# One half of a batch's shared network moved behind the routed experts, with the guards off `tensor_scalar` and new instruction lists

## The chip, the cores and the metric

The kernel runs on one core of one Trainium2 chip. The metric is the device time of one execution in microseconds (us); lower is better. Before the change the median of three runs is 598.0 us (597.97 to 598.31).

## What is computed

`x` holds four batches (B = 4) of 512 tokens with 512 features. Two layers follow one another, each behind a layer norm and each added back to `x` with the tanh of a gate:

```python
x = x + tanh(g_xattn) * expert_forward(layernorm(x), fside, ctx)     # per batch, weights of its own
x = x + tanh(g_ffn)   * moe(layernorm(x), gate_w, w_gate, w_up, w_down, ws_gate, ws_up, ws_down)

def expert_forward(xe, guw, dw):          # twice a "smooth quant" linear: int8 steps per row
    gate, up = split(smooth_quant_linear(xe, guw)); return smooth_quant_linear(silu(gate) * up, dw)

def moe(x):                               # T = 2048 tokens, E = 16 experts, top 2, capacity 256, I = 352
    w, idx = top_k(softmax(x @ gate_w.T), 2)
    y  = for each expert: (silu(buf @ w_gate) * (buf @ w_up)) @ w_down, rows added back with w
    sh = (silu(x @ ws_gate) * (x @ ws_up)) @ ws_down                  # the shared network, IS = 704
    return y + sh
```

In the smooth-quant linear the maxima over columns give `s = sqrt(max(amax_x, eps) / max(amax_w, eps))`, the maxima over rows give the step sizes `max(row_max, eps) / 127`, and `eps` is 1e-6.

## The kernel before

Every engine has a program of its own, a list of calls that is written out by hand; nothing reorders it. Semaphores tie the lists together: a call waits at its head, and everything behind it on that engine waits with it. So the order of these five lists is the schedule.

**Stage A, the quantised layer (calls that end in `_a`, `_b`, `w`, `w2`, with a batch number first).** For a batch `a`, PE turns weights and tokens into the PSUM banks `ps_a` (`turn_w`, `turn_x`), DVE reduces their maxima (`amax_w`, `amax_x`), `ratio_a`, POOL's `root_a` and `smooth_a` make the smoothing, `scale_x` (DVE) and `scale_w` (POOL, 128x2048) apply it, `x_steps` and `w_steps` make the steps, ACT quantises (`quant_x`, `quant_w`) and moves the turned integers (`ints_x`, `ints_w`), and PE multiplies (`product_a`, `dequant_a` on DVE behind it). The second linear repeats this in `ps_d` with half the width (`turn_w2`, `turn_g`, `root_b`, `scale_g`, `scale_w2`, `product_b`, `dequant_b`). `add_x`, `stats_b`, POOL's `norm_b` and ACT's `normalise_b` then give the batch's second layer norm `y`, which is stored to `x2n_scratch` and turned (`turn_y`, `x_hi`, `x_lo`) for the router (`logits`, `turn_logits`, `top_two`, ...). `stats_a(a)` on DVE and `norm_a(a)` on POOL are the first layer norm of batch `a`. POOL also makes the low parts of the shared weights (`split_gu_lo`, `split_d_lo`).

**The guards.** The three `max(.., eps)` are `tensor_scalar` instructions on 2 or 4 columns: in `ratio` (L1065, `recip_w`), in `smoothing` (L1086) and in `step_size` (L1100, `x_step` from PSUM, `w_step` from SBUF).

**Full precision.** A product in float32 is made of three in a reduced form: `three` issues hi*hi, hi*lo and lo*hi. So each weight and each activation is split into a high part (ACT) and a low part (DVE or POOL).

**The shared network.** It goes by half-batches of 256 tokens, `shared_up(b, h, m, g)` and `shared_down(b, h, m, k)` in six chunks m (five of 128 columns of IS, one of 64 in which gate and up share one product). A half is 11 calls of `shared_up` with 12 matmuls of 256 columns each, and 12 calls of `shared_down` (10 with 3 matmuls of 512 columns, 2 with 2). Behind each chunk stand `shared_silu` and `shared_hi` on ACT and `shared_hid` and `shared_lo` on DVE. Six halves, (0,0) to (2,1), are woven into stage A by the lists. Where PE would have nothing to do, `keep_busy(n)` issues n matmuls that nobody reads (L1752).

**The experts.** When the routing tables are ready (`index`), POOL gathers an expert's tokens (`gather`), PE turns them (`turn_tokens`, L1938), and 16 equal steps follow: three `up` of 24 matmuls of 256 columns, three `down` of 6 of 512 columns, one `turn_tokens`. SP may load expert 1's weights only when all shared up-products are done (`sp.wait_ge(sh_gu, CHUNKS)`), since they lie over the shared weights.

**The tail.** The two halves of the last batch run as four more steps of the same kind, E to E + 3: the shared weights are loaded in two parts of 352 columns as if they were two experts (E and E + 1 in the weight buffers), and each part is multiplied with each half (`weights_of`). `shared_rows(e)` on DVE adds each step's rows to `x2`. When all expert rows are in `expert_out_scratch`, POOL's `gather_rows(b, k)` fetches them for each batch (L554, 8 gathers per batch), `add_rows(b, half)` on DVE adds them (L1666, L1671), and SP stores `x2` (L396).

Of the kernel before, what the change touches and what calls it, by code (L numbers as in the profile page):

```python
# [24 lines left out]
def flamingo_block(nc, x, guw, dw, g_x, g_f, gate_w, w_gate, w_up, w_down, s_gate, s_up, s_down, out):  # L25
# [63 lines left out]
    slot_col = place(cur, "slot_col", [P, 2, J, 2], U32)  # L89
# [102 lines left out]
    HALVES = 2 * (B - 1)  # L192
    CHUNKS = MS * HALVES
    NE, NW = E + 4, E + 2

    def weights_of(e):

        return e if e < E else E + (e - E) // 2
# [13 lines left out]
    with ExitStack() as ctx:  # L212
        def sem(name):
# [47 lines left out]
        slot_cols, got_in, sum_half, summed, out_done = (  # L261
            sem("slot_cols"), [[sem(f"got_in{k}_{half}") for half in "ab"] for k in range(3)], sem("sum_half"), sem("summed"), sem("out_done"))
# [23 lines left out]
        def _(sp):  # L286
# [98 lines left out]
            load_tokens(E, 0)  # L385
# [11 lines left out]
            sp.wait_ge(out_done, 16 * 2 * B)  # L397
# [3 lines left out]
        def _(pool):  # L401
# [4 lines left out]
            pool.memset(ln_eps[:], LN_EPS).then_inc(const_ready, 1)  # L406
            pool.memset(zeros[:], 0.0).then_inc(const_ready, 1)
# [8 lines left out]
            pool.wait_ge(const_ready, 11)  # L416
# [9 lines left out]
            def norm(b, done, mean, var, var_eps, rstd, mean_rstd, shift):  # L426

                pool.tensor_tensor(var_eps, var, ln_eps[:], ALU.add).then_inc(done, 1)
# [5 lines left out]
                pool.tensor_tensor(shift, zeros[:], mean_rstd, ALU.subtract).then_inc(done, 1)  # L434
# [19 lines left out]
            def root_a(a):  # L454
                root(LA, a, C)
# [33 lines left out]
            root_a(0)  # L489
            norm_a(1)  # L490
            scale_w(0)
            norm_a(2)
            split_gu_lo(0)
            norm_a(3)
            split_gu_lo(1)
            split_gu_lo(2)
            split_gu_lo(3)
            split_d_lo(0)
            root_b(0)
            split_d_lo(1)  # L500
# [1866 lines left out]
```

## Time and profile before

| | before |
|---|---|
| median of 3 runs | 598.0 us |
| the profiled execution | 599.84 us |
| its span, first to last instruction | 598.1 us |
| mean granted clock of TensorE | 0.981 of full speed |
| PE, DVE, ACT, POOL busy | 94%, 70%, 50%, 26% |
| experts' steps, matmuls of 256 columns | about 282 ns each as shown |

The profile shows each instruction with its own length; matmuls overlap one another, so the distance from one step to the same place in the next tells PE's pace, and the mean of one matmul doesn't. An idle engine is shown with what released it. The chain of waits follows the end of the span back, step by step.

### The profile page before, as it was taken

What the parts mean: (1) busy time and instruction counts of PE and PEld (TensorE: products, weight loads), DVE (VectorE), ACT (ScalarE), POOL (GpSimd) and SP (SyncE); (2) the same over time, 40 slices, a digit from 0 to 9 for tenths busy, and PEclk for the clock granted to TensorE, in tenths of its full rate; (3) what the DMA queues carried; (4) which work ended last, traced back from release to release, by engine and by line L of the source; (5) the groups of instructions that cost most, each with busy time, mean ns of one, the idle gap of its engine ahead of it and who ended that gap; (6) DMA issues with size and microseconds to landing.
All of it is one profiled execution on the core that took longest, in us unless ns stands there. A gap on an engine that the chain in (4) does not pass through costs nothing.

```text
span 598.1 us, 10333 instructions
## 1 busy us (share of the span) xinstructions
PE 560.9 (94%) x3949; PEld 478.8 (80%) x3949; DVE 415.8 (70%) x755; ACT 296.1 (50%) x460; POOL 156.9 (26%) x157
## 2 busy tenths in 40 slices
PE   7977989999998999999998999999999999999991
PEld 3544647988896888888887899999999999999980
DVE  4868796997899757566826766665666666666586
ACT  3175574386338541543146556556556666653110
POOL 2469510231041101010041222222232220006772
PEclk9979899999999999999999999999999999999995
DMA  7911021013001120011076667777777765755686
GB/s 261 385 48 64 13 94 71 2 36 141 1 2 37 70 98 2 1 71 50 2 243 188 216 219 239 232 261 239 248 248 231 232 215 181 231 206 154 199 279 241
DMA packets 45460, 89.01 MB, mean 149 GB/s; under 512 B 4256, under 2 KB 24736, under 8 KB 44400
## 3 DMA queue, kind: packets, MB, share of 16 engines
q1 hardware_dynamic: 40304, 71.74, 35.5%
q0 software_dynamic: 5120, 16.78, 9.2%
q8 instruction: 24, 0.39, 0.3%
q14 instruction: 12, 0.10, 0.1%
HBM read 71.73 MB, written 16.78 MB: 148 GB/s over the span
## 4 chain that ended last, share of the span: by engine, by line
PE 66%; DVE 14%; POOL 6%; DMA 5%; issue 4%; ACT 4%; SPq 1%; POOLq 0%; DVEq 0%; ACTq 0%
PE ps_gu L1710 12%; PE ps_gu L1711 11%; PE ps_gu L1712 11%; POOL got L554 5%; PE ps_d L1710 5%; PE ps_d L1711 5%; PE ps_d L1712 5%; PE ps_a L1938 2%; PE ps_d L1731 2%; DMA raw_d<-in_L_ffn_w_down 2%; PE ps_a L1731 2%; PE ps_a L1799 2%; DMA w<-in_ctx 2%; PE ps_gu L1752 1%; DVE xn L1119 1%
## 5 line engine op out<-in xcount | busy, mean ns | idle before, releaser
L1710 PE MATMUL ps_gu<-ex_xhi,w_hi 128*128 128x256 f32 (+1 forms) x480 | 136.9, 285 | 1.7 <-DVE w_lo L1321 1.7
L1711 PE MATMUL ps_gu<-ex_xlo,w_hi 128*128 128x256 f32 (+1 forms) x480 | 135.0, 281 | 0.0
L1712 PE MATMUL ps_gu<-ex_xhi,w_lo 128*128 128x256 f32 (+1 forms) x480 | 134.8, 281 | 0.0
L1710 PEld LDWEIGHTS ps_gu<-ex_xhi,w_hi 128*128 128x128 f32 (+1 forms) x480 | 86.3, 180 | 6.7 <-issue 5.6
L1711 PEld LDWEIGHTS ps_gu<-ex_xlo,w_hi 128*128 128x128 f32 (+1 forms) x480 | 86.1, 179 | 1.2
L1712 PEld LDWEIGHTS ps_gu<-ex_xhi,w_lo 128*128 128x128 f32 (+1 forms) x480 | 86.3, 180 | 0.0
L1710 PE MATMUL ps_gu<-xt_hi,sw_hi 128*128 128x256 f32 x264 | 78.7, 298 | 1.0 <-DVE sh_hid L1293 1.0
L1711 PE MATMUL ps_gu<-xt_lo,sw_hi 128*128 128x256 f32 x264 | 74.4, 282 | 0.0
L1712 PE MATMUL ps_gu<-xt_hi,sw_lo 128*128 128x256 f32 x264 | 74.4, 282 | 0.0
L1321 DVE TENSOR_TENSOR w_lo<-raw_gu,w_hi 128x1408 fp32r<-128x1408 f32 x36 | 58.2, 1616 | 1.1 <-DMA x2n_scratch<-y 1.1
L1710 PEld LDWEIGHTS ps_gu<-xt_hi,sw_hi 128*128 128x128 f32 x264 | 50.0, 190 | 5.4 <-DVE sh_hid L1293 1.7
L934 ACT ACTIVATE ex_silu<-ps_gu 128x256 f32<-128x256 f32 (+1 forms) x60 | 22.5, 375 | 60.5 <-PE ps_gu L1712 60.5
L525 POOL DMA_INDIRECT xg<-x2n_scratch,idx_col x32 | 47.1, 1473 | 17.6 <-POOL idx_col L521 12.7
L1710 PE MATMUL ps_d<-wd_hi,ex_hhi 128*128 128x512 f32 (+1 forms) x120 | 47.7, 398 | 3.7 <-DVE ex_hlo L1606 3.7
L1711 PEld LDWEIGHTS ps_gu<-xt_lo,sw_hi 128*128 128x128 f32 x264 | 50.2, 190 | 1.1
L938 ACT ACTIVATE ex_hhi<-ex_hid 128x256 fp32r<-128x256 f32 (+1 forms) x60 | 25.1, 418 | 50.7 <-DVE ex_hid L1603 50.7
L1712 PEld LDWEIGHTS ps_gu<-xt_hi,sw_lo 128*128 128x128 f32 x264 | 50.2, 190 | 0.0
L1752 PE MATMUL ps_gu<-ident_b 128*128 128x512 bf16 x157 | 44.9, 412 | 3.6 <-POOL fold L424 3.6
L1712 PE MATMUL ps_d<-wd_hi,ex_hlo 128*128 128x512 f32 (+1 forms) x120 | 47.6, 397 | 0.0
L1711 PE MATMUL ps_d<-wd_lo,ex_hhi 128*128 128x512 f32 (+1 forms) x120 | 47.5, 396 | 0.0
L1606 DVE TENSOR_TENSOR ex_hlo<-ex_hid,ex_hhi 128x256 fp32r<-128x256 f32 (+1 forms) x60 | 25.4, 424 | 30.9 <-ACT ex_hhi L938 30.9
L741 ACT ACTIVATE w_hi<-raw_gu 128x2816 fp32r<-128x2816 f32 x18 | 45.8, 2547 | 0.3 <-DMA raw_d<-in_L_ffn_w_down 0.3
(217 smaller groups left out, 1129.3 us busy)
## 6 DMA issues: line engine op xcount, KB each, us to landing
raw_gu<-in_L_ffn_w_gate SPq DMA_DIRECT2D x16, 704.0 KB, 4.5
raw_gu<-in_L_ffn_w_up SPq DMA_DIRECT2D x16, 704.0 KB, 6.0
raw_d<-in_L_ffn_w_down SPq DMA_DIRECT2D x16, 512.0 KB, 7.3
expert_out_scratch<-eo SPq DMA_DIRECT2D x16, 512.0 KB, 7.5
w<-in_fside_BxS2xS SPq DMA_DIRECT2D x4, 1024.0 KB, 5.2
x2n_scratch<-y SPq DMA_DIRECT2D x4, 1024.0 KB, 3.8
out<-x SPq DMA_DIRECT2D x8, 512.0 KB, 4.7
x<-in_x SPq DMA_DIRECT2D x1, 3072.0 KB, 16.7
```

The costliest lines, as they stand in the source:

```text
L525: pool.indirect_dma_start(xg[q][:, h, :], None, x2n_dram, bass.IndirectOffsetOnAxis(idx_col[:, q, h:h + 1], 0)).then_inc(xg_in[q], 16)
L554: pool.indirect_dma_start(got[k][:, j, n, :], None, eo_dram, bass.IndirectOffsetOnAxis(slot_col[:, b % 2, j, n:n + 1], 0)).then_inc(got_in ...
L741: act.activation(w_hi[q][:], raw_gu[q][:], ACT.Copy).then_inc(ex_whi, 1)
L934: act.activation(ex_silu[0:k, (q + m) % 2, :], ps_gu[0:k, (q + m) % 2, 0:CAP], ACT.Silu).then_inc(ex_sg, 1)
L938: act.activation(ex_hhi[0:k, m, :], ex_hid[0:k, (q + m) % 2, :], ACT.Copy).then_inc(ex_hi, 1)
L1321: dve.tensor_tensor(w_lo[q][:, g], raw_gu[q][:, g], w_hi[q][:, g].bitcast(F32), ALU.subtract).then_inc(ex_wlo, 1)
L1606: dve.tensor_tensor(ex_hlo[0:k, m, :], ex_hid[0:k, (q + m) % 2, :], ex_hhi[0:k, m, :].bitcast(F32), ALU.subtract).then_inc(ex_lo, 1)
L1710: pe.matmul(dst, a_hi, b_hi, start=start, stop=False)
L1711: pe.matmul(dst, a_hi, b_lo, start=False, stop=False)
L1712: return pe.matmul(dst, a_lo, b_hi, start=False, stop=stop)
L1731: last = pe.transpose(dst[:, j * P:(j + 1) * P], src[:, j, c * P:(c + 1) * P], ident[:])
L1752: pe.matmul(ps_gu[:, 1, :], ident_b[:], ident_b[:].unsqueeze(1).broadcast_to((P, J, P)), start=True, stop=True)
```

## The change

What it does:

- The shared network's half (2,0) leaves the lists of stage A. It is done behind the experts, with the last batch's two halves: `TAIL = [(2,0), (3,0), (3,1)]`. Five halves stay in stage A.
- The tail goes by half-batch: for each of three halves the two parts of the weights follow one another and add up in the same PSUM banks, so that the tail has six steps, and `shared_rows` adds each half's rows once instead of twice.
- The last batch's expert rows are added row tile by row tile, ahead of the last half's shared rows, and its output is stored in four parts.
- The guards are `scalar_tensor_tensor` with a second operand (`ones`, or a constant tile with 1/127) in place of `tensor_scalar`.
- The slot columns of all batches are copied once, ahead of the row gathers.
- The lists of all engines are new, with 135 matmuls in `keep_busy` where there were 157.

```diff
-    HALVES = 2 * (B - 1)
+    TAIL = [(B - 2, 0), (B - 1, 0), (B - 1, 1)]
+    HALVES = 2 * B - len(TAIL)
...
-    NE, NW = E + 4, E + 2
+    NE, NW = E + 2 * len(TAIL), E + 2
...
+            def at_least_eps(dst, src, factor):
+
+                return dve.scalar_tensor_tensor(out=dst, in0=src, scalar=Q_EPS, in1=factor, op0=ALU.max, op1=ALU.mult)
...
-                link(dve.tensor_scalar(w, sm["amax_w"][:, 0:width], Q_EPS, None, ALU.max))
+                link(at_least_eps(w, sm["amax_w"][:, 0:width], ones[:, 0:width]))
...
-                return dve.tensor_scalar(small[layer][which + "_step"][:], row_max, Q_EPS, 1.0 / QMAX, ALU.max, ALU.mult)
+                return at_least_eps(small[layer][which + "_step"][:], row_max, inv_qmax)
...
             root_a(0)
+            scale_w(0)
+            split_gu_lo(0)
             norm_a(1)
-            scale_w(0)
+            split_gu_lo(1)
             norm_a(2)
...
+            def last_rows():
+
+                t = len(TAIL) - 1
+                b, h = TAIL[t]
+                dve.wait_ge(ex_d, M * NE)
+                dve.wait_ge(sum_last, HALF)
+                for k in range(HALF):
+                    j = HALF * h + k
+                    dve.scalar_tensor_tensor(out=x2[:, b, j, :], in0=ps_d[:, 2 * (t % 2) + k, :], scalar=tg[:, 1:2],
+                                             in1=x2[:, b, j, :], op0=ALU.mult, op1=ALU.add).then_inc(summed, 1)
...
+            for t in range(len(TAIL)):
+                for w in range(2):
+                    tail_up(t, w, 0)
+                    if w:
+                        tail_down(t, 0, 2)
+                    elif t:
+                        tail_down(t - 1, 1, 2)
+                    else:
+                        down(E - 1, 1, 2)
+                    tail_up(t, w, 1)
+                    tail_down(t, w, 0)
+                    if w and t + 1 < len(TAIL):
+                        turn_tokens(E + t + 1, E // 2, (t + 1) % 2)
+                    tail_up(t, w, 2)
+                    tail_down(t, w, 1)
+            tail_down(len(TAIL) - 1, 1, 2)
```

DVE's list at the first batch's stage A, from the first maxima to the first steps (`bn_a` is `stats_a`, `amax_w_b` is `amax_w2`). Before:

```order
L1035 TENSOR_REDUCE amax_w_b<-ps_d 128x1 x2
L1035 TENSOR_REDUCE amax_x_a<-ps_a 128x1 x4
L1088 RECIPROCAL rsmooth_a<-smooth_a 128x4
L1012 BN_STATS bn_a<-x_49 128x6 x4
L1119 TENSOR_TENSOR xn<-xn,ps_a 128x2048
L1097 TENSOR_REDUCE ps_a<-xn 128x4
L1100 TENSOR_SCALAR x_step_a<-ps_a 128x4
L1012 BN_STATS bn_a<-x_49 128x6 x4
L1097 TENSOR_REDUCE w_max_a<-w_120 128x4
L1100 TENSOR_SCALAR w_step_a<-w_max_a 128x4
```

The same place in the changed kernel:

```order
L1035 TENSOR_REDUCE amax_x_a<-ps_a 128x1 x4
L1092 RECIPROCAL rsmooth_a<-smooth_a 128x4
L1123 TENSOR_TENSOR xn<-xn,ps_a 128x2048
L1101 TENSOR_REDUCE ps_a<-xn 128x4
L1063 SCALAR_TENSOR_TENSOR x_step_a<-ps_a,consts 128x4
L1101 TENSOR_REDUCE w_max_a<-w_118 128x4
L1063 SCALAR_TENSOR_TENSOR w_step_a<-w_max_a,consts 128x4
L1035 TENSOR_REDUCE amax_w_b<-ps_d 128x1
L1012 BN_STATS bn_a<-x_49 128x6 x4
```

The maxima of `w2` and the statistics of batches 1 and 2 now stand behind the first steps, and the guards have another form.

DVE's list at the very end (`x_49` is the result `x2`, `got_172` is a batch's gathered rows, `ex_hid` and `ex_hlo` belong to the last step's last chunk). Before:

```order
L1603 TENSOR_TENSOR ex_hid<-ex_silu,ps_gu 96x256
L1606 TENSOR_TENSOR ex_hlo<-ex_hid,ex_hhi 96x256
L1666 SCALAR_TENSOR_TENSOR x_49<-got_174,wts,x_49 128x512 x2
L1671 SCALAR_TENSOR_TENSOR x_49<-got_174,wts,x_49 128x512 x2
L1657 SCALAR_TENSOR_TENSOR x_49<-ps_d,tg,x_49 128x512 x2
L1666 SCALAR_TENSOR_TENSOR x_49<-got_172,wts,x_49 128x512 x2
L1671 SCALAR_TENSOR_TENSOR x_49<-got_172,wts,x_49 128x512 x2
```

The same place in the changed kernel:

```order
L1594 TENSOR_TENSOR ex_hid<-ex_silu,ps_gu 96x256
L1597 TENSOR_TENSOR ex_hlo<-ex_hid,ex_hhi 96x256
L1665 SCALAR_TENSOR_TENSOR x_49<-got_170,wts,x_49 128x512
L1668 SCALAR_TENSOR_TENSOR x_49<-got_170,wts,x_49 128x512
L1665 SCALAR_TENSOR_TENSOR x_49<-got_170,wts,x_49 128x512
L1668 SCALAR_TENSOR_TENSOR x_49<-got_170,wts,x_49 128x512
L1659 SCALAR_TENSOR_TENSOR x_49<-ps_d,tg,x_49 128x512 x2
```

Before, the last batch's gathered rows came behind the last shared rows (twice the last two lines); now the shared rows come last.

## Rows read from the trace of the kernel before

**Rows 1.** Stages: us, PE, PEld, DVE, ACT, POOL busy (x), PEclk, DMA, GB/s.

```profile
0.00:101.20 101.20, 84.05 (x490) 49.80 (x490) 75.04 (x133) 53.22 (x74) 45.15 (x51) 0.95 0.39 139
101.20:278.30 177.10, 174.45 (x1302) 151.36 (x1302) 137.08 (x299) 87.73 (x163) 25.57 (x22) 1.00 0.12 43
278.30:309.50 31.20, 30.66 (x224) 26.37 (x223) 19.37 (x65) 9.26 (x18) 6.56 (x9) 1.00 0.22 67
309.50:530.50 221.00, 217.58 (x1563) 201.76 (x1562) 139.02 (x186) 128.68 (x173) 43.53 (x39) 1.00 0.72 234
530.50:598.10 67.60, 54.12 (x375) 49.51 (x374) 45.32 (x73) 17.24 (x32) 36.12 (x36) 0.91 0.63 199
```

**Rows 2.** The chain of waits in order of time: start us, us, what.

```profile
322.47 1.53 DVE w_lo L1321
...
348.38 0.87 PE ps_a L1938 x8
...
525.55 0.89 PE ps_a L1938 x8
```

**Rows 3.** Timeline of DVE in stage A: start us, us, engine, line, instruction.

```profile
13.86 1.34 DVE L1035 TENSOR_REDUCE amax_w_b<-ps_d 128x1 f32<-128x512 f32 x2 [0.69 <-PE ps_d L1731]
...
20.86 2.47 DVE L1012 BATCH_NORM_STATS2 bn_a<-x 128x6 f32<-128x512 f32 x4
...
31.43 2.25 DVE L1097 TENSOR_REDUCE w_max_a<-w 128x4 f32<-128x2048 f32 x1
...
33.71 2.84 DVE L1100 TENSOR_SCALAR w_step_a<-w_max_a 128x4 f32<-128x4 f32 x1
...
55.56 2.75 DVE L1065 TENSOR_SCALAR recip_w_b<-amax_w_b 128x2 f32<-128x2 f32 x1
...
123.24 3.04 DVE L1301 TENSOR_TENSOR sh_hlo<-sh_hid,sh_hhi 128x256 fp32r<-128x256 f32 x1
```

**Rows 4.** Timeline of POOL in stage A.

```profile
25.62 4.53 POOL L463 TENSOR_TENSOR w<-w,line_a 128x2048 f32<-128x2048 f32 x1
...
33.38 3.15 POOL L475 TENSOR_TENSOR sw_lo<-raw_sgu,sw_hi 128x1408 fp32r<-128x1408 f32 x1
...
51.68 6.61 POOL L482 TENSOR_TENSOR sd_lo<-raw_sd,sd_hi 128x2560 fp32r<-128x2560 f32 x1
...
121.38 4.62 POOL L463 TENSOR_TENSOR w<-w,line_a 128x2048 f32<-128x2048 f32 x1 [5.27 <-ACT line_a L625]
```

**Rows 5.** Timeline of ACT in stage A.

```profile
23.25 0.60 ACT L625 ACTIVATE line_a<-ps_a 128x512 f32<-128x512 f32 x1 [7.84 <-PE ps_a L1746]
...
39.74 1.36 ACT L590 ACTIVATE sw_hi<-raw_sgu 128x1408 fp32r<-128x1408 f32 x1
...
92.48 2.93 ACT L607 ACTIVATE xn<-x,shift_a,rstd_a 128x512 f32<-128x512 f32 x4
```

**Rows 6.** Timeline of all engines where the experts begin.

```profile
298.38 0.18 DVE L1283 CAST idx<-r_tmp 128x32 uint32<-128x32 f32 x1
...
304.92 1.09 PE L1938 MATMUL ps_a<-ident,xg 128*128 128x128 f32 x8 [0.54 <-DMA xg<-x2n_scratch,idx_col]
...
309.51 0.38 PE L1710 MATMUL ps_gu<-ex_xhi,w_hi 128*128 128x256 f32 x1
```

**Rows 7.** Timeline of the tail: up-products, gathers, last chunk, last sum (first and last).

```profile
530.53 0.36 PE L1710 MATMUL ps_gu<-ex_xhi,w_hi 128*128 128x256 f32 x1
...
541.06 0.97 POOL L554 DMA_INDIRECT got<-expert_out_scratch,slot_col  x1 [0.84 <-POOL slot_col L549]
...
580.78 0.28 PE L1712 MATMUL ps_gu<-ex_xhi,w_lo 128*96 128x256 f32 x1
...
583.96 0.42 DVE L1606 TENSOR_TENSOR ex_hlo<-ex_hid,ex_hhi 96x256 fp32r<-96x256 f32 x1 [0.48 <-ACT ex_hhi L938]
...
586.83 1.14 POOL L554 DMA_INDIRECT got<-expert_out_scratch,slot_col  x1 [0.30 <-issue]
...
593.49 1.42 DVE L1671 SCALAR_TENSOR_TENSOR x<-got,wts,x 128x512 f32<-128x512 f32 x2
```

More of the change, by code:

```diff
@@ L503, in _ @@
             scale_w(1)
+            split_gu_lo(2)
             norm_b(0)
+            split_d_lo(0)
+            split_gu_lo(3)
+            split_d_lo(1)
+            norm_a(3)
+            root_b(1)
             root_a(2)
-            root_b(1)
             scale_w2(1)
@@ L977, in _ @@
             for e in range(E + 1, NE):
-                for m in range(M):
-                    hidden(e, e % 2, m, False)
+                t = (e - E) // 2 + 1
+                hidden(e, e % 2, 0, False)
+                hidden(e, e % 2, 1, False)
+                if e % 2 and t < len(TAIL):
+                    tokens(E + t, t % 2)
+                hidden(e, e % 2, 2, False)
         @block.vector
@@ L1988, in _ @@
             turn_g(0, 1)
-            keep_busy(6)
+            turn_w(1, 3)
+            keep_busy(4)
             turn_x(1, 0)
@@ L2009, in _ @@
             product_b(0, 1)
+            keep_busy(5)
+            turn_qx(1, 0)
             keep_busy(1)
@@ L2017, in _ @@
             row_w(1)
-            keep_busy(7)
+            keep_busy(1)
             turn_qw(1, 0)
@@ L2099, in _ @@
-            turn_y(1, 3)
-            shared_down(0, 0, 4, 0)
-            turn_w(3, 2)
-            shared_down(0, 0, 4, 1)
-            logits(1)
-            turn_w(3, 3)
-            shared_down(0, 0, 5, 0)
-            turn_x(3, 0)
-            turn_logits(1)
+            shared_down(0, 0, 5, 1)
+            turn_x(3, 0)
+            shared_up(0, 1, 3, 0)
+            table(0)
+            shared_up(0, 1, 3, 1)
+            turn_w2(2, 0)
+            shared_down(0, 1, 0, 0)
+            turn_w2(2, 1)
@@ L2166, in _ @@
+            turn_y(2, 1)
+            product_a(3, 0)
+            turn_y(2, 2)
+            shared_down(1, 0, 0, 1)
+            turn_y(2, 3)
+            shared_down(1, 0, 1, 0)
+            product_a(3, 1)
+            logits(2)
+            product_a(3, 2)
+            turn_logits(2)
+            shared_down(1, 0, 1, 1)
             product_a(3, 3)
-            turn_y(2, 1)
+            rank(1)
             shared_up(1, 0, 5, 0)
-            turn_y(2, 2)
             shared_up(1, 1, 0, 0)
-            turn_y(2, 3)
+            shared_down(1, 0, 2, 0)
```

882 lines of the change are left out of this document (420 added, 462 removed).

## The prediction

> **What bounds the kernel now.** I read busy time by stage first, then the chain of waits, then timelines at the places that the new lists change.
>
> There are four stages [rows 1]; the edges at 101.2 and 278.3 us are the first and the last batch's `turn_logits`. Up to 101.2 us PE is busy 84 us, but much of that is `keep_busy`: this is the latency of stage A's first batch, before any shared product can start. From there to 309.5 us PE is busy 205 of 208 us. From 309.5 us the experts, again PE alone, with DVE at 63%. At 530.5 us the last expert's step is over but for one down-product, and the tail begins.
>
> PE's pace comes from the chain: from 348.38 to 525.55 us there are 13 experts' steps [rows 2], so 13.63 us each, of which the turn of the tokens is 0.87. The other 12.76 us are 72 matmuls of 256 columns and 18 of 512, 108 units of 256 columns, so **0.118 us a unit**. The 282 ns that the profile gives a matmul is its length, not its pace.
>
> The end isn't PE's. The tail's last up-product is at 580.9 us [rows 7], but POOL is still issuing gathers until 588, and DVE's last sum ends at 594.9, 3.2 us ahead of the span's end [rows 1, 7]. From 530.5 us to the end pass 67.6 us.
>
> **The tail grows.** A half in the tail is two parts of 108 units, 25.5 us, and 0.87 for turning its tokens where it isn't the first. Before, the tail's up-products took 50.4 us [rows 7], which is 4 x 12.76 + 0.87 less the last 1.38 of down-products: no stall in it. With six steps it is 6 x 12.76 + 2 x 0.87 - 1.38 = 76.9 us. Behind it come the last chunk's hidden values (about 2.0 us, an estimate: four instructions like the 0.42 of `ex_hlo`, three gaps up to its 0.48), the last batch's row tiles 2 and 3 (four sums, two of which take 1.42 by the last row of [rows 7], with a wait between the two of a tile: 3.0), the last shared rows (1.4) and the same 3.2 for the store: 9.7. So the end lies 86.7 us behind the start of the tail instead of 67.6: **+19.1 us**. The 32 gathers, issued from 541.06 to 588 [rows 7], are covered by PE's own work now; that is why 26.4 us more on PE lengthen the tail by 19.1 only. Were they late after all, DVE would stop ahead of `hidden` and PE with it; they have some 8 us in hand, since the last gather should land some 60 us into the tail and its first sum stands 68 us into it. The single copy of the slot columns takes three copies off POOL under that cover: nothing. The extra load of tokens on SP (512 KB) stands behind the experts' stores and ahead of the output: nothing.
>
> **Stage A loses one half.** `shared_up` of a half is 132 units, `shared_down` 34 matmuls of 512 columns, 68 units: 200 units, 23.6 us, in a stretch that PE fills. The lists pull `turn_x` of batch 2 (12 turns of 0.11) from in front of this stretch into it: +1.4. So **-22.2 us** if PE stays as full as it is. It won't quite. DVE is busy 137 of the 177 us up to 278.3 [rows 1], and with a half less it has about 5 us less work in 22 less. The PE idle that this adds isn't in the trace: its bounds are 0, and all 22.2 (DVE and the latencies set the stretch already). The row nearest to it, PE 98.5% busy in the old lists, lies at the first end; I take 4.2.
> At the end of the stretch one wait can be counted. The routing needs about 13.5 us from the last `turn_logits` to the index, and 6.5 from the index to the turn of expert 0's tokens (298.38 to 304.92, [rows 6]). From the last `turn_logits` PE's old list had 255 units' worth, 30 us, the new one has 18, of which some 16 stand ahead of the turn. PE waits there 2.3 us more. Together +6.5.
>
> **The first batch's chain gets shorter.** In the new DVE list the first steps come at once [rows 3 to 5]:
> - `amax_w2` (two reductions) no longer stands ahead of `amax_x`: -1.3.
> - `scale_w(0)` on POOL began at 25.62 though ACT had copied its row at 23.85 [rows 5]: it stood behind `norm_a(1)`, which waits for `stats_a(1)` on DVE. Now -1.8. `w_max` began 1.3 behind its end, held by `stats_a(2)`: -1.3.
> - `w_step_a` took 2.84 us for four columns, until POOL's low part of the shared weights ended at 36.53. In the new POOL list nothing is on POOL then: -2.7. `recip_w_b` took 2.75, until 58.3, where POOL's 6.61 us ended: -2.6.
> - `split_gu_hi` (1.36) no longer stands ahead of `ints_w`, and fewer matmuls of `keep_busy` stand there: -1.7.
> - `silu_a(1)` and `normalise_a(2)`, which held the batch's last two turned chunks (92.48, 2.93 us), come behind them: -2.9. Small gains between: -0.4.
>
> The sum is **-14.7 us**, so the shared products begin near 85 us. What follows them is POOL's last `split_gu_lo`, due at the same time by the same rows, so there is little more to have here.
>
> **The guards.** `sh_hlo`, a `tensor_tensor` with two SBUF inputs and no fast form, took 3.04 us instead of 0.4 and ended at 126.28, just behind POOL's 4.62 us that ended at 126.00 [rows 3, 4]. So two SBUF inputs are enough to wait for POOL, and the new guard of `w_step` and `recip_w` has two. I give the new form nothing; the 5.3 us above come from the new order alone. `x_step` reads PSUM and never waited.
> The Trainium skill says the same (GPSIMD Engine Reference, Specifications and Key points): POOL shares its SBUF interfaces with VectorE, and instructions in a two-port mode or with two SBUF inputs contend. By a rule that only the two-port mode contends, every guard would be free, and the sum would be about 3 us lower, for one more stall, of 2.7, in the middle stretch; row and page speak against it.
>
> **Expert 1's weights.** They may be loaded when the shared up-products are over. Their low part ended at 324.0 [rows 2], while expert 0's step, 13.63 us from 309.51 less the 1.4 of its last down-product, would have let expert 1 start at 321.7. Since the 2.3 us wait above now lies behind the last up-product, this wait goes: **-2.3**.
>
> **Sum.** -14.7 - 22.2 + 6.5 - 2.3 + 19.1 = -13.6 us, so the span goes from 598.1 to 584.5 us. The profiled execution took 599.84, 1.74 more than its span: 586.2 after. The runs' median, 598.0, lies 0.3% below it, which gives **584.4 us**.
>
> **Rivals.**
> - *The lists are worse than they look: PE waits more in the middle stretch.* For: DVE at 77% there, tighter with less to fill; new POOL orders may put `scale_w` (4.6 us) over the guard of `w_step_b` in batches 1 to 3, up to 2.8 each, like the stall of `w_step_a` [rows 3]. Against: PE has other work queued for most of it. 9 us more: 593.
> - *The front doesn't get shorter* (a load or POOL's splits set it), but the middle does: without the 14.7 the time is 599.1, no change. For: POOL's `split_d_lo` and `split_gu_lo(3)` end only then. Against: each term is a row. A part of it is likelier than the whole.
> - *The middle stretch keeps its length, set by stage A's own latencies* (slower). The 22.2 us come back as PE idle, the tail's 19.1 stay, the front gives 14.7: -14.7 + 0 + 19.1 - 2.3 + 2.3 = +4.4, 602.4 us. It decides where PE's added idle passes 20 us. Against: PE is full there now, and DVE has 40 us free.
> - *More than I count*: no added idle in the middle and the wait for the tokens hidden: 578.
>
> **Chances.** Forecast as reckoned 0.55, better by 4 us or more 0.15, the first rival 0.17, the second 0.05, the third 0.06, something else slower 0.02. Below 0.2% a measurement of this kernel can't tell a difference. So faster 0.89, within 0.2% 0.03, slower 0.08. The range takes in the better case and most of the first rival: 576 to 596 us.
>
> **What the changed profile would show.** Right: the first `turn_logits` near 87 us; `w_step_a` at 0.2 us near 29; the first expert's matmul near 279; tail steps of 12.76 us without stalls; the last sums on DVE reading PSUM. Wrong: PE's share of 100 to 275 us clearly under 97%; a two-input guard of over 2 us on the chain; gathers still being issued when the last up-product ends; the first expert later than 290 us.

## The result, and the profile after

| | before | after |
|---|---|---|
| median of 19 runs each, us | 598.16 | 595.54 |
| lowest to highest | 597.73 to 600.37 | 593.04 to 597.62 |
| profiled execution: span, mean granted clock | 598.1, 0.981 | 595.7, 0.982 |

The ratio is 0.9951, with a 95% interval from 0.994 to 0.9962: faster, by 0.5% where 2.3% were forecast, 11.1 us above the forecast 584.4. On the four chips of all later runs the kernel before takes 609 us, and the changed kernel 616 on the one where it was repeated unaltered: there the change is a loss (`r_after` below).

The same five stages in the trace of the changed kernel, to set beside [rows 1]; columns: stretch, us, then busy us (and instructions) of PE, PEld, DVE, ACT, POOL, then the granted clock, DMA share, GB/s:

```profile
0.00:92.90 92.90, 75.43 (x456) 45.06 (x456) 71.08 (x128) 50.56 (x70) 44.18 (x49) 0.96 0.43 151
92.90:259.30 166.40, 163.41 (x1225) 140.11 (x1224) 134.65 (x297) 84.89 (x159) 27.75 (x26) 1.00 0.13 46
259.30:288.10 28.80, 22.39 (x149) 17.73 (x148) 15.71 (x57) 7.27 (x13) 7.44 (x9) 0.88 0.38 122
288.10:509.90 221.80, 218.83 (x1564) 203.03 (x1563) 140.82 (x188) 128.54 (x173) 46.26 (x40) 0.99 0.70 227
509.90:595.70 85.80, 79.83 (x563) 73.93 (x562) 50.99 (x84) 23.07 (x45) 35.41 (x32) 0.98 0.52 164
```

Against the forecast's stages: the front lasts 92.9 us instead of 86.5 (+6.4); from the first `turn_logits` to the first expert's matmul 195.2 instead of 192.7 (+2.5); the experts 221.8 instead of 218.7 (+3.1); the tail 85.8 instead of 86.7 (-0.9). These make up the 11.1. Three places hold the excess.

**The front: the stalls moved.** DVE's timeline of the changed kernel there (start us, us, engine, line, instruction), at the guards and the gating:

```profile
29.43 0.16 DVE L1063 SCALAR_TENSOR_TENSOR w_step_a<-w_max_a,consts 128x4 f32<-128x4 f32 x1
...
42.56 4.14 DVE L1178 TENSOR_TENSOR gated<-gated,xn 128x1024 f32<-128x1024 f32 x1 [0.56 <-ACT gated L668]
...
57.30 2.29 DVE L1063 SCALAR_TENSOR_TENSOR smooth_a<-root_a,ones 128x4 f32<-128x4 f32 x1
...
68.19 2.29 DVE L1101 TENSOR_REDUCE w_max_a<-w 128x4 f32<-128x2048 f32 x1 [0.44 <-POOL w L469]
...
70.51 0.81 DVE L1063 SCALAR_TENSOR_TENSOR w_step_a<-w_max_a,consts 128x4 f32<-128x4 f32 x1
```

And POOL's timeline at the same moments:

```profile
42.47 3.15 POOL L481 TENSOR_TENSOR sw_lo<-raw_sgu,sw_hi 128x1408 fp32r<-128x1408 f32 x1
45.58 1.18 POOL L434 TENSOR_TENSOR var_a<-mv_a,consts 128x4 f32<-128x4 f32 x1
...
57.24 2.34 POOL L475 TENSOR_TENSOR w<-w,line_b 128x1024 f32<-128x1024 f32 x1
...
68.13 3.17 POOL L481 TENSOR_TENSOR sw_lo<-raw_sgu,sw_hi 128x1408 fp32r<-128x1408 f32 x1
```

The first `w_step_a` is free now, as forecast (2.84 in [rows 3]). But the gating multiply, 1.2 us long in the three other batches, stands under the second `split_gu_lo`, and the guard of `smooth_a`, which had never waited before, under the scaling of the down weights. The multiply was long in the kernel before too, 2.10 us, so that 2.0 of its 2.9 us are new. Its line there:

```profile
50.71 2.10 DVE L1174 TENSOR_TENSOR gated<-gated,xn 128x1024 f32<-128x1024 f32 x1
```

Behind the multiply PE's granted clock is 0.50 from about 46 to 52 us. That isn't new either: in the kernel before it averages 0.66 from 34 to 44 us, behind the old stall of `w_step_a`.

`w_max_a`, a reduction with one input, ran its usual 2.29 us wholly under POOL's operation: not every instruction waits.

**The tokens of expert 0.** The chain there, in order of time:

```profile
273.65 2.10 POOL xg L531
276.06 6.17 DMA xg<-x2n_scratch,idx_col
282.27 1.97 PE ps_a L1957 x8
```

And the index on DVE and the loads on SP's queue, from the timeline:

```profile
272.22 0.18 DVE L1287 CAST idx<-r_tmp 128x32 uint32<-128x32 f32 x1
...
274.52 0.37 SPq L310 DMA_DIRECT2D raw_gu<-in_L_ffn_w_gate  x1
274.93 0.51 SPq L311 DMA_DIRECT2D raw_gu<-in_L_ffn_w_up  x1
275.48 0.51 SPq L314 DMA_DIRECT2D raw_d<-in_L_ffn_w_down  x1
276.03 0.83 SPq L316 DMA_DIRECT2D raw_d<-in_L_ffn_w_down  x1
```

The index is ready 12.9 us behind the last `turn_logits` (13.5 reckoned). But SP now asks for expert 1's weights at 274.5, 2.3 us behind the index, because the shared up-products end earlier against the routing; in the kernel before it asked at 303.7, 5.3 us behind. So the token rows share the DMA engines with the weights: 10.05 us from the index to the turn, not 6.5 [rows 6]. The windows show the second half of the bill (columns as above):

```profile
276.70:282.20 5.50, 0.40 (x2) 0.00 (x0) 0.00 (x0) 0.00 (x0) 2.41 (x4) 0.91 1.05 385
282.20:291.30 9.10, 9.03 (x30) 6.87 (x31) 4.29 (x5) 2.72 (x3) 2.10 (x3) 0.50 0.55 165
291.30:302.00 10.70, 10.38 (x78) 9.69 (x78) 4.37 (x8) 6.51 (x8) 2.44 (x2) 0.99 0.63 202
```

PE stands for 5 us, and the clock granted afterwards averages 0.50, 1.2 GHz, over 9 us.

**Expert 1's weights** are still waited for: `w_lo` at 302.07 is on the chain, as at 322.47 before [rows 2].

### The profile page after: what moved, and what is told of

Read it like the earlier page. It is cut to its first block, busy times and chain, and to the rows that moved or that the text cites. A ratio compares the mean times of both kernels' runs of the same rounds, so it can differ in the third digit from the quotient of the medians.

```text
span 595.7 us, 10318 instructions
## 1 busy us (share of the span) xinstructions
PE 559.9 (94%) x3949; PEld 479.9 (81%) x3949; DVE 413.2 (69%) x752; ACT 294.3 (49%) x460; POOL 161.0 (27%) x155
## 4 chain that ended last, share of the span: by engine, by line
PE 74%; DVE 15%; ACT 5%; POOL 2%; issue 2%; DMA 1%; DVEq 0%; POOLq 0%; ACTq 0%
PE ps_gu L1729 13%; PE ps_gu L1730 13%; PE ps_gu L1731 13%; PE ps_d L1729 6%; PE ps_d L1731 6%; PE ps_d L1730 6%; PE ps_a L1957 3%; PE ps_d L1750 2%; PE ps_gu L1771 2%; PE ps_a L1750 2%; PE ps_a L1818 1%; DMA xg<-x2n_scratch,idx_col 1%; ACT y L709 1%; PE ps_d L1818 1%; DVE pos_oh L1269 1%
## 5 line engine op out<-in xcount | busy, mean ns | idle before, releaser
L1729 PE MATMUL ps_gu<-ex_xhi,w_hi 128*128 128x256 f32 (+1 forms) x528 | 151.3, 287 | 1.3 <-DVE w_lo L1325 1.3
L1730 PE MATMUL ps_gu<-ex_xlo,w_hi 128*128 128x256 f32 (+1 forms) x528 | 149.3, 283 | 0.0
L1731 PE MATMUL ps_gu<-ex_xhi,w_lo 128*128 128x256 f32 (+1 forms) x528 | 148.8, 282 | 0.0
L1729 PE MATMUL ps_gu<-xt_hi,sw_hi 128*128 128x256 f32 x220 | 65.5, 298 | 0.0
L531 POOL DMA_INDIRECT xg<-x2n_scratch,idx_col x32 | 50.3, 1571 | 17.6 <-POOL idx_col L527 12.7
L1729 PE MATMUL ps_d<-wd_hi,ex_hhi 128*128 128x512 f32 x132 | 52.2, 395 | 2.1 <-DVE ex_hlo L1597 2.1
L1594 DVE TENSOR_TENSOR ex_hid<-ex_silu,ps_gu 128x256 f32<-128x256 f32 (+1 forms) x66 | 27.6, 419 | 35.4 <-ACT ex_silu L929 34.5
L1731 PE MATMUL ps_d<-wd_hi,ex_hlo 128*128 128x512 f32 x132 | 52.1, 395 | 0.0
L1730 PE MATMUL ps_d<-wd_lo,ex_hhi 128*128 128x512 f32 x132 | 52.0, 394 | 0.0
L561 POOL DMA_INDIRECT got<-expert_out_scratch,slot_col x32 | 35.4, 1106 | 59.8 <-DMA expert_out_scratch<-eo 50.3
L1341 DVE TENSOR_TENSOR ex_xlo<-ps_a,ex_xhi 128x1024 fp32r<-128x1024 f32 x19 | 23.3, 1224 | 34.1 <-ACT ex_xhi L761 34.1
```

What stands on the lines that cost most here:

```text
L531: pool.indirect_dma_start(xg[q][:, h, :], None, x2n_dram, bass.IndirectOffsetOnAxis(idx_col[:, q, h:h + 1], 0)).then_inc(xg_in[q], 16)
L561: pool.indirect_dma_start(got[k][:, j, n, :], None, eo_dram, bass.IndirectOffsetOnAxis(slot_col[:, b, j, n:n + 1], 0)).then_inc(got_in[k][ ...
L1594: dve.tensor_tensor(ex_hid[0:k, (q + m) % 2, :], ex_silu[0:k, (q + m) % 2, :], ps_gu[0:k, (q + m) % 2, CAP:2 * CAP], ALU.mult).then_inc(ex ...
L1729: pe.matmul(dst, a_hi, b_hi, start=start, stop=False)
L1730: pe.matmul(dst, a_hi, b_lo, start=False, stop=False)
L1731: return pe.matmul(dst, a_lo, b_hi, start=False, stop=stop)
```

## The experiments

Each kernel ran beside the kernel before on one chip, in five rounds. A run is called by the first part of its label (e1, f4, h2). All were run where the kernel before takes 608.5 to 609.8 us, so absolute times are not to be set against 595.5. The places where batches and experts pass can be, since up to the tail `r_after` repeats the first trace within 0.1 us. They are read from one trace of each run (starts on PE, us; medians and ratios are of all its executions):

| | first turn_logits | last | expert 0's tokens | expert 2's | tail's first | span's end | median | ratio to before |
|---|---|---|---|---|---|---|---|---|
| before, first chip | 101.1 | 278.3 | 304.9 | 334.5 | 525.4 | 598.1 | 598.2 | |
| after, first chip | 92.9 | 259.3 | 282.3 | 314.1 | 504.7 | 595.7 | 595.5 | 0.995 |
| r_before | 100.8 | 278.0 | 304.6 | 333.9 | 524.9 | 609.2 | 609.9 | 1.000 |
| r_after | 92.9 | 259.4 | 282.3 | 314.2 | 504.8 | 616.8 | 616.4 | 1.010 |
| e1 | 92.3 | 258.8 | 279.1 | 310.7 | 501.3 | 614.4 | 615.2 | 1.008 |
| e2 | 91.6 | 258.1 | 282.3 | 311.6 | 502.2 | 614.6 | 616.0 | 1.010 |
| e3 | 91.7 | 258.1 | 282.4 | 312.0 | 502.6 | 614.8 | 615.1 | 1.009 |
| e4 | 100.5 | 275.3 | 302.1 | 332.0 | 522.6 | 635.8 | 636.0 | 1.043 |
| e6 | 86.8 | 251.5 | 274.5 | 303.8 | 494.4 | 606.5 | 609.0 | 0.999 |
| e7 | 89.4 | 255.8 | 278.7 | 310.4 | 501.0 | 610.5 | 611.2 | 1.004 |
| e8 | 86.6 | 251.4 | 271.8 | 303.8 | 494.4 | 606.4 | 608.0 | 0.997 |
| f4 | 86.7 | 251.5 | 272.4 | 301.8 | 492.4 | 600.9 | 604.5 | 0.994 |
| f2 | 87.6 | 252.3 | 275.4 | 305.0 | 495.6 | 594.9 | 596.7 | 0.982 |
| f1 | 87.5 | 252.3 | 275.8 | 305.2 | 495.8 | 587.0 | 588.1 | 0.967 |
| h2 | 93.0 | 259.4 | 283.7 | 313.5 | 504.1 | 595.3 | 595.1 | 0.976 |
| h3 | 86.6 | 251.3 | 272.2 | 303.0 | 493.6 | 584.8 | 586.6 | 0.962 |
| h5 | 98.8 | 273.7 | 300.3 | 330.2 | 520.9 | 612.1 | 614.1 | 1.009 |

How far can one trace be trusted? The front's lists are the same in `r_after`, e1, e2 and h2, and their first `turn_logits` stands at 91.6 to 93.0; with e6's front it stands at 86.6 to 87.6 in six traces. From the last `turn_logits` to expert 2's tokens, a stretch that none of them alters, pass 53.9 to 54.8 us in `r_after`, e3, e7 and h2, and 52.3 to 52.9 in e6, f1 and f2. A difference of about 1 us between two traces shows nothing.

### The change itself on the second kind of chip: r_after, r_before

No edit.

> The changed kernel itself, unaltered, on the chip that the other runs of this call get. In the last four runs (on a chip where the kernel before takes 609.8 us, not 598.2) PE stood for 20 us in the tail between single matmuls, with nothing that it waited for, while the row gathers of batches 0 and 1 ran. Theory (the chip, or the moment, does it, and the four edits have no part in it): on the same kind of chip the unaltered change shows that stop as well, and its time there is above the kernel before's, some 612 us; where the kernel before takes 598, there is no stop and it takes 595.5. Rival (the edits shifted PE's code against the gathers): no stop in the unaltered change on any chip, 0.995 of the kernel before.

> The kernel before, unaltered, for its trace on this chip: the ratio is 1.000. Where the kernel before takes 609.8 us: the theory that PE stops for want of instructions while rows are gathered says that its extra 11.6 us lie in its tail, as one stop during a batch's gathers; the rival says that they are spread over the whole span (a slower memory), a few per cent of every stage that waits for DMA.

From the tail's first tokens to the end the changed kernel takes 91.0 us on the first chip and 112.0 here; the kernel before 72.7 and 84.3. The tail of `r_after` in windows:

```profile
504.78:520.50 15.72, 15.72 (x117) 14.70 (x116) 10.42 (x13) 8.25 (x12) 0.00 (x0) 1.00 0.58 194
520.50:537.60 17.10, 16.99 (x122) 15.66 (x120) 5.67 (x10) 4.90 (x9) 13.42 (x13) 1.00 0.63 182
537.60:556.90 19.30, 6.39 (x18) 3.98 (x17) 0.96 (x3) 1.06 (x3) 10.39 (x11) 0.58 0.60 173
556.90:616.80 59.90, 53.05 (x350) 48.27 (x350) 37.10 (x63) 10.25 (x24) 7.71 (x8) 0.93 0.30 106
```

And PE in the third of them:

```profile
543.82 0.37 PE L1731 MATMUL ps_gu<-ex_xhi,w_lo 128*128 128x256 f32 x1 [0.85 <-issue]
545.21 0.57 PE L1729 MATMUL ps_gu<-ex_xhi,w_hi 128*128 128x256 f32 x1 [1.02 <-issue]
546.61 0.37 PE L1730 MATMUL ps_gu<-ex_xlo,w_hi 128*128 128x256 f32 x1 [0.82 <-issue]
548.71 0.37 PE L1731 MATMUL ps_gu<-ex_xhi,w_lo 128*128 128x256 f32 x1 [1.72 <-issue]
```

The gathers begin at 520.5, one each 1.25 us, 24 without a pause. After 17 us of them PE starts recorded matmuls mostly only every 0.7 to 2 us instead of every 0.12, "issue" being idle time for which the profile shows no awaited event; it recovers at 556.9, some 5 us behind the last of the 24. So the edits don't do it, and the first theory holds: the chip or the moment does, and no run tells these two apart. In `r_before` it begins 22 us behind the first gather (540.5) and is shorter. The gathers there come in runs of eight with a pause of 1 us between them, which doesn't prevent it; its windows:

```profile
538.60:562.60 24.00, 24.00 (x175) 22.63 (x174) 9.52 (x15) 5.78 (x12) 17.09 (x19) 1.00 0.57 163
562.60:575.50 12.90, 6.29 (x20) 3.69 (x18) 4.99 (x8) 0.80 (x2) 7.58 (x8) 0.85 0.68 194
```

Which DMA queues moved anything during the stop of `r_after` (537.6 to 556.9), packets, MB, share:

```profile
q0 software_dynamic: 1023, 3.34, 60.1%
```

and in the same window of the changed kernel on the first chip, where PE is full:

```profile
q0 software_dynamic: 1063, 3.49, 65.2%
q1 hardware_dynamic: 282, 1.04, 13.5%
q8 instruction: 1, 0.02, 0.3%
```

So the gathers are about as fast here as there, and no queue moves instructions during the stop.

PE's slow starts are only half of it. ACT's timeline around the stop, on the first chip:

```profile
535.05 0.38 ACT L929 ACTIVATE ex_silu<-ps_gu 96x256 f32<-96x256 f32 x1 [1.80 <-PE ps_gu L1731]
```

and in `r_after`:

```profile
555.05 0.38 ACT L929 ACTIVATE ex_silu<-ps_gu 96x256 f32<-96x256 f32 x1 [20.23 <-remote]
```

In both PE starts the last product that this instruction needs at 534.7 to 534.8, before the slow starts. On the first chip ACT follows 0.3 us later, here 20.3. ACT itself isn't late: by the trace's semaphore records, of which some are missing, PE's signal for these products came at 555.02 (535.03 there). PE's next down-product needs what ACT and DVE make of them, and stands at 556.84 instead of 539.08. So PE's signals come late as well as its starts. The same wait is 20.4 us in e4 and in e6, 7.1 and 9.5 in `r_before`; in h2, with paced gathers, ACT follows within 2.6 us, and on the first chip within 1.6.

### Expert 1's weights behind expert 0's tokens: e1

```diff
             sp.wait_ge(sh_gu, CHUNKS)
+            sp.wait_ge(xg_in[0], 32)
             load_raw(1, 1)
```

> The changed kernel, with expert 1's weights asked for on SP only once expert 0's token rows have landed. Theory (the token rows and the 1.8 MB of weights share the DMA engines, and PE's idle 5.3 us let the clock fall): from the table of token indices being ready to the first token transpose about 6.5 us, as in the kernel before, in place of 10.05; PE idle under 2.5 us there; the granted clock stays 1.00 where it was 0.50 from 282 to 291; the first expert matmul 3.5 to 6 us earlier; the time 4 us below the changed kernel's 595.5, so 591.5 (590 to 593), unless the weights, which land some 4 us later, are then waited for at expert 1. Rival (the gather is slow by itself, its issues on POOL or its descriptors): the first token transpose still 9 us or more after the indices, the clock still at 0.50, and 595.5 to 599.

The gather lands after 3.46 us (6.17 unaltered), and the turn stands 7.35 us behind the index instead of 9.98: the contention is real. The clock didn't do as expected: it still averages 0.65 from 279 to 283 us and 0.75 from 283 to 291. Up to expert 2's tokens 51.9 us pass from the last `turn_logits`, 2.0 to 2.9 us less than in the four traces without the hold (53.9 to 54.8).

### Filler matmuls in the wait: e2

```diff
+            pe.wait_ge(sh_h, CHUNKS)
+            keep_busy(20)
             turn_tokens(0, 0, 0)
```

> The changed kernel, with 20 filler matmuls (0.21 us each, 4.3 us) on PE ahead of expert 0's token transposes; the weights are asked for where they were. Theory (half of what was lost at this place is the clock and not the wait): the tokens still arrive at the same time, 10 us after the indices, but the granted clock stays 1.00 from 282 to 291, where 9.3 us of work at 0.50 took twice its time; less what waits for ACT and DVE there, 3 us off, so 592.5 (591 to 594). Rival (the stretch is bound by the splitting of the tokens and by the weights of expert 1, so the clock costs nothing that the next waits don't hide): 595.5, within 1 us.

The clock from 282.2 to 291.3 us is 0.81 instead of 0.50, and expert 2's tokens come 53.5 us behind the last `turn_logits` instead of 54.8. But e3, which is without the filler, has nearly the same: its tokens come at the same 24.2 us, the clock of this window is 0.77, and expert 2's tokens stand at 53.9. So the filler's gain isn't shown, and neither are the 3 us expected of it; the median shows none. What e3 and `r_after` do show side by side, at the same edits here: with the clock at 0.77 the step from expert 0's tokens to expert 1's takes 12.8 us, at 0.50 it takes 15.1 (the loads were asked for 1 us earlier in e3, so not all of this need be the clock).

### The guards back as tensor_scalar: e3

```diff
-                return dve.scalar_tensor_tensor(out=dst, in0=src, scalar=Q_EPS, in1=factor, op0=ALU.max, op1=ALU.mult)
+                return dve.tensor_scalar(dst, src, Q_EPS, factor, ALU.max, *([ALU.mult] if factor else []))
...
```

> The changed kernel with its guards as tensor_scalar again, lists as they are. Theory (DVE's operation waits for the end of POOL's long one in either form, and the new lists have other guards under POOL's operations): the smoothing guards at 57.3 and 107.4 take 2.3 us as now, the first logits transpose is at 92.9 within 1 us, and the ratio to the changed kernel is 1.000 within 0.002. Rival (the new form waits less, and is what brought part of the 8.3 us of the front): two or more guards take 1 to 3 us that take 0.16 now, the first logits transpose at 95 or later, and 2 us or more slower than the changed kernel.

From the timeline of e3:

```profile
56.10 2.30 DVE L1063 TENSOR_SCALAR smooth_a<-root_a 128x4 f32<-128x4 f32 x1
```

2.30 us in the old form, 2.29 in the new one; the second `w_step_a` 0.81 and 0.80. The form is worth nothing in either direction. The front is 1.2 us shorter than in `r_after`, more than the 1 us expected, but so it is in e2, which has the new form: 91.6. The guards' times are the same; after the stall of the gating multiply the clock recovers earlier in both (48 to 53 us: 0.72 in e2 and e3, 0.54 in `r_after`).

### The lists of the kernel before: e4, and h5 with paced gathers

The changed kernel's tail, tables and guards, and the five lists of the kernel before without the moved half's parts:

```diff
-            shared_up(2, 0, 0, 0)
-            shared_down(2, 0, 0, 0)
-            shared_silu(2, 0, 0)
-            shared_hid(2, 0, 0)
...
```

> The move alone: the tail of the changed kernel (six steps, rows added once) and its guards, but PE, DVE, ACT, POOL and SP work through the lists of the kernel before, from which the twelve parts of the moved half-batch are struck. Theory (the first 101 us are paid by the new lists alone, and the moved half's work was what filled the waits of the middle): the first logits transpose stays at 101 us, where the new lists have 92.9; the middle loses 10 to 18 of its 177 us, the tail is 85.8; 602 us (599 to 607), slower than the kernel before. Rival (the move brings the gain and the new lists little): 596 or less.

> e4 (the new tail and guards with the lists of the kernel before, the moved half struck) with paced gathers. e4 took 636.0 us, 20 of them PE's stop; its tail began at 522.6, 2.8 us ahead of the kernel before's 525.4, where the new lists brought 20.7. Theory (with the old lists the struck work had filled waits, and the tail of 91 us is paid in full): 522.6 + 91 and what lies around the span, 615 (613 to 618); so the new lists are worth 18 to 19 us. Rival (part of e4's 636 is not the stop): 620 or more.

The middle stretch in the windows of e4:

```profile
100.50:275.30 174.80, 157.50 (x1143) 133.91 (x1148) 132.46 (x287) 82.68 (x150) 25.43 (x22) 0.95 0.13 43
```

The tail begins 2.8 us earlier than before, where some 22 us of PE's work were taken out: 17.3 of 174.8 us are PE idle now (2.7 before), at a clock of 0.95. The theory's 10 to 18 us off the middle didn't come; the stretch lost 2.3 (177.1 before). Without the stop, h5 takes 614.1, so the move alone costs 5.4 us even against a kernel before that loses some 11 to its own; with the new lists it is h2's 595.1, 19.0 us less.

### POOL's order in the front: e6, e7

```diff
             norm_a(1)
-            split_gu_lo(1)
             norm_a(2)
+            split_gu_lo(1)
```

e6 also has, in `scale_w2`:

```diff
                 pool.wait_ge(row_s_b_done, b + 1)
+                if b + 1 < B:
+                    pool.wait_ge(smooth_ready[LA], 2 * b + 4)
```

> The changed kernel with two edits on POOL's list: the low half of the second shared piece after the norm of batch 2 (in place of before it), and the scaling of the next down weights held until DVE has its smoothing factors. Theory (DVE's operations with two SBUF inputs wait for the whole of POOL's long operation, and these two waits are on the path of the first 93 us): the gating multiply at 42.6 takes 1.2 us in place of 4.14, the smoothing guards at 57.3 and 107.4 0.16 in place of 2.3; the first logits transpose 4 to 5 us earlier, at 88 to 89; 591 us (589.5 to 592.5). Rival (another chain, the weights' transposes on PE, ends in these stretches at the same time): the two operations are short, but the first logits transpose moves under 1.5 us, and 594 to 596.

> The changed kernel with only the first of e6's two edits: the norm of batch 2 ahead of the low half of the second shared piece, so that the gating multiply at 42.6 doesn't meet POOL's 3.15 us. e6 moved the first logits transpose from 92.9 to 86.8. Theory (the multiply's 2.9 us are paid with interest: PE was idle for 3.1 us and its clock at 0.50 from 46 to 53 us): the first logits transpose at 88.5 to 89.5, 4 us of the 6.1 from this edit, no stretch at 0.50 behind 44 us. Rival (each stall costs what it lasts and the rest came with the second edit): 90 to 90.5. The smoothing guard stays at 2.3 us in both.

From e6's timeline:

```profile
42.58 1.23 DVE L1180 TENSOR_TENSOR gated<-gated,xn 128x1024 f32<-128x1024 f32 x1 [0.57 <-ACT gated L670]
...
46.71 1.66 DVE L1065 SCALAR_TENSOR_TENSOR recip_w_b<-amax_w_b,ones 128x2 f32<-128x2 f32 x1
...
53.35 0.16 DVE L1065 SCALAR_TENSOR_TENSOR smooth_a<-root_a,ones 128x4 f32<-128x4 f32 x1
```

Both stalls are gone, and a guard that was free in the changed kernel (`recip_w_b`, 0.15 at 50.65) now waits 1.5 us under the operation that was moved.

The stretch from 48 to 53 us in the windows of `r_after`:

```profile
48.00:53.00 5.00, 5.00 (x21) 3.61 (x20) 2.78 (x7) 4.02 (x4) 1.07 (x3) 0.54 0.00 0
```

and in those of e7:

```profile
48.00:53.00 5.00, 3.91 (x26) 2.60 (x25) 4.70 (x13) 1.25 (x2) 1.74 (x3) 1.00 0.00 0
```

e7 brings 3.5 us (89.4 where 92.9 stood), inside the theory's range. But unaltered fronts stand at 91.6 to 93.0, so that it is 2.3 to 3.6, and theory and rival aren't told apart. Nor did the clock stay up: it averages 0.76 from 53 to 60 us, where `r_after` has 1.00. So what the half clock costs in the front is not shown. e6 brings 6.1 at the first batch (4.0 to 6.4 by the spread) and, by the guard at 107.4, another 1.7 in the middle (164.7 us from the first to the last `turn_logits` instead of 166.4).

### Both, and the weights held in part: e8, f4

e8 is e6 with e1's hold. f4 is e6 with:

```diff
-            load_raw(1, 1)
+            sp.dma_start(raw_gu[1][:, 0], wg_v[1]).then_inc(raw_in[1], 16)
+            sp.wait_ge(xg_in[0], 32)
+            sp.dma_start(raw_gu[1][:, 1], wu_v[1]).then_inc(raw_in[1], 16)
+            load_d(1, w_down[1])
```

> The two edits of e6 (POOL's order in the front) and the one of e1 (expert 1's weights asked for once expert 0's tokens are there) together. Theory (they act on stages one behind the other, so they add): first logits transpose at 86.8 and the last at 251.5 as in e6, the second expert's token transposes 33.7 us behind that (e1 had 34.2, the changed kernel 38.0), so 9 to 10 us below the changed kernel of this call: 586 us where that takes 595.5, if the tail has no stop. Rival (the hold of the weights costs expert 1 what it gives expert 0): 6 us below the changed kernel, as e6 alone.

> e6 with three of expert 1's four weight loads held until expert 0's token rows are there (the gate weights go out at once). e8 held all four: tokens 2.5 us earlier, but expert 1's own weights then 3.5 us later, and nothing left at expert 2. Theory (both need the same DMA bytes before expert 1 can start, so the order only shares the wait out): the third experts' token transposes 51 to 52.5 us behind the last logits transpose (52.3 in e6, 52.4 in e8), within 1.5 us of e6's time. Rival (the first load fills the DMA engines while POOL still writes the gather's descriptors, for free): 50 or less, 2 us or more below e6.

e8's rival was right: tokens 2.6 us earlier, and nothing left at expert 2 (52.4 us against 52.3 in e6). f4's rival was nearer than its theory: the tokens come nearly as early (272.4), and expert 2's stand 50.3 us behind, 2.0 us better than e6. h3, with the same hold, has 51.6, so the gain is 1 to 2 us: queueing one load early and three late keeps something of both.

### The gathers of the tail paced: f1, f2, h2, h3

```diff
             def gather_rows(b, k):
                 for j in range(J):
+                    pool.wait_ge(ex_d, M * E + 3 + 3 * (J * b + j) // 4)
```

That is f1, on e6; h2 has it alone on the changed kernel; h3 on f4. f2, on e6, has instead one wait ahead of batch 1's gathers (`M * E + 6`) and one ahead of batch 2's (`M * E + 10`).

> e6 (the changed kernel with POOL's two edits in the front) with the row gathers of the tail paced: each pair of gathers waits on POOL until PE has finished one more down projection, three in four of them, so that 2.5 us of gathers stand in every 3.2. Theory (PE's stop of 20 us comes from the unbroken run of 24 gathers; it began 17 us after the first of them in the unaltered change): with pauses no stop or one under 5 us, the tail from its first token transposes to the end 91 to 95 us in place of 112, and 590 (587 to 594) on a chip where the kernel before takes 609.7. Rival (the total of the gathers matters and not how closely they follow one another): the stop is as long and only later, 607 to 610.

> e6 with the row gathers in bursts: batch 1's eight wait for the seventh down projection of the tail and batch 2's for the eleventh, so that 5 us or more lie between one burst of 10 us and the next. Theory (unbroken run): as f1, no stop, since none of the bursts reaches the 17 us after which PE stopped; 590 (587 to 594). Rival 1 (each burst stops PE at a code page's end, by chance): one or two stops of 5 to 8 us, 597 to 605. Rival 2 (rows late for the sums): no stop, but DVE's adding of batch 2 or 3 waits and the end is 5 us later.

> The changed kernel with paced row gathers and no other edit. Theory (the stop in the tail is a thing by itself, and front, middle and experts stay as in the unaltered change): first logits transpose at 92.9, tail from its first token transposes 91 us in place of 112, 595 to 597 whatever the chip, so 0.978 of the kernel before where that takes 609, 0.995 where it takes 598. Rival (pacing also lengthens the tail where nothing stopped): 598 or more.

> The paced gathers, POOL's two edits in the front and expert 1's weights held but for the gate weights, together: f1 with f4's hold. Theory (stages one behind the other add): f1's 588.1 less the 2.0 us that f4 won up to the third experts' token transposes, 586 (585 to 587.5). Rival (the tail's first step meets something later, such as the last experts' stores, that gives it back): 588 or more.

The windows of f1, from the tail's first tokens:

```profile
495.80:518.90 23.10, 23.10 (x167) 21.54 (x166) 14.03 (x19) 11.31 (x18) 0.00 (x0) 1.00 0.41 139
518.90:570.00 51.10, 51.10 (x368) 47.85 (x367) 28.67 (x50) 11.13 (x25) 34.06 (x32) 1.00 0.69 208
570.00:587.00 17.00, 10.97 (x70) 9.32 (x68) 11.31 (x19) 2.02 (x5) 1.30 (x1) 0.88 0.33 120
```

All 32 gathers in 51 us, and PE full throughout. h2 takes 595.1 us where the kernel before takes 608.7, the same time as the change had on the first chip, so the stop was all that differed, and the pauses cost nothing. f2 has its longest stop at 566 us, where ACT's instruction came 4.7 us behind its products, late in the only run of 16 gathers left (550.7 to 572); its window:

```profile
565.00:575.00 10.00, 6.30 (x28) 4.89 (x27) 4.00 (x7) 1.54 (x4) 5.35 (x6) 0.72 0.79 238
```

That fits the length of the run. But in `r_before` the stop came although no run was longer than eight, with 1 us between them. So what is shown is that PE stopped 16 to 22 us into a stretch of dense gathers and that f1's pauses avert it; whether the unbroken run is what counts, or the rate of the gathers, is open. h3, with everything, takes **586.6 us**, 0.9624 of the kernel before (0.9608 to 0.964); it was tried only where that takes 609. It is the best version here.

## Why the prediction missed, point by point

- *The front, -14.7, measured -8.3.* The terms read from rows came (the first `w_step_a` 0.16 us at 29.43). The step that failed is the count of stalls: "the 5.3 us above come from the new order alone" took off the old ones and put in none. The new order adds 2.0 us at `gated` (4.14 where 2.10 stood), 2.1 at `smooth_a` and 0.65 at the second `w_step_a`, 4.8 of the missing 6.4; for the other 1.6 no cause is shown. One of the profile's signs of being wrong came with them, a two-input guard of over 2 us on the chain (`smooth_a`). With the two larger ones lifted and a new one of 1.5 in their place (e6), the first `turn_logits` stands at 86.8, where 87 was forecast.
- *The guards' form, nothing.* Right (e3). So is what the Trainium skill says under GPSIMD Engine Reference, Specifications and Key points, of two SBUF inputs: `gated` agrees, 4.14 us in place of 1.2.
- *The middle, -22.2 + 4.2.* PE's idle time there is 3.0 us in 166.4, after 2.7 in 177.1: hardly any was added, and 4.2 was too much. The work taken out came to what was reckoned: up to the first expert's matmul PE is busy 185.8 us instead of 205.1, and 22.2 us less if the 5.8 us that it worked at half clock (282.3 to 288.1) are counted as 2.9 (an estimate). The rival in which the stretch keeps its length is what e4 shows, with 17.3 us idle: it is the new lists that avert it.
- *The wait for the tokens, +2.3.* This is the term that fell furthest. The 6.5 us from index to turn were carried over, though the load of expert 1's weights had moved to the same moment; they became 10.05 (e1: 3.5 of DMA time instead of 6.2), and the half clock behind it was not in the sum at all. PE's idle time there grew by 5.9 us (6.4 of 28.8 us after 0.5 of 31.2), and the half clock takes some 2.9 more up to the first expert's matmul (the same estimate): 8.8 where 2.3 stood. With the 4.2 not needed, that leaves the 2.5 up to there, within some tenths. The 2.3 itself doesn't follow from the 20.0 us of routing and "some 16" of work that the text gives; the trace has 17.8 us of work there (259.3 to 277.1), which would give it.
- *Expert 1's weights, -2.3.* They didn't go: the load is asked for earlier, but tokens and weights need the same DMA engines, so that one wait split in two. The experts' 3.1 us above the forecast are mostly this 2.3; the last 3 us at half clock lie there too.
- *The tail, +19.1.* Right to 0.9 us on the first chip (85.8 against 86.7), the gathers covered (the last at 562.9, the last up-product at 586.4), the last sums on PSUM. Its four parts behind the last up-product add up to 9.6, not 9.7, which changes nothing. "Covered by PE's own work" was wrong on the others: there PE stops while POOL issues gathers without a pause, and the tail is 21 us longer; h2's pauses bring them back. No view of the first chip's trace shows it.

Rivals: the first (593, more waits than they look) named the right kind of mechanism, stalls under new POOL orders, at the wrong place, for the middle stretch and not for the front. That 595.5 lies just inside the range of 576 to 596 is luck: the upper part of the range was meant for waits that didn't come.

## What to carry to other kernels

After a reorder, don't only strike the collisions that go: lay each long POOL operation of the new order over DVE's list and look at what it meets now, and do the same for each load that a shorter queue issues sooner. An idle gap on PE of 3 to 5 us can cost more than its length, since the clock granted behind it was 0.50 for 3 to 10 us in these traces. Dense indirect gathers beside a busy PE want pauses (609.0 to 588.1 us on the chips used here, e6 and f1), and a kernel that is to run on more than one chip wants measuring on more than one.

## What was not expected of the hardware

- Two kinds of chip, as it seems (the first was not used again, so a change with time isn't excluded): up to the tail the traces agree within 0.6 us, and then the same kernel takes 598.2 or 609.9 (before), 595.5 or 616.4 (after). Shown: the loss lies in the gathers' time and goes with pauses. The products of PE start slowly there, and its signal for products started before comes some 20 us late (`r_after`, e4, e6). Not shown: why. The Trainium skill (Runtime: NRT & Kernel Launch, Instruction fetch mechanics) says that each engine fetches its code by a DMA queue of its own in blocks of 16 KiB, mostly hidden. Code that comes late behind the gathers would look like this, but the trace speaks against it: the first chip's tail shows such blocks of 16 KB on queue q8 at 511.8, 529.7, 547.3 and 565.0, and `r_after` at 512.4, 530.8 and 567.0, none in the stop, so that no block's arrival ends it; and what came late was also the signal of products that PE had already started. The cause stays open.
- A reduction with one SBUF input ran 2.29 us under a POOL operation without delay, while a guard of four columns waited 2.3 us for its end, in either form.
- POOL's small operations wait too: `var_a`, 0.19 us at 40.69, took 1.18 at 45.58, until `gated` ended at 46.70.
